# A change to the first pair of images, and to the place of three additions, in a normalised-attention block in f32

## What is computed

```python
y = group_norm(x)                             # 32 groups, no affine part
q, k = conv1x1_bn(y, qw, ...), conv1x1_bn(y, kw, ...)   # 8 heads of 32
v4 = conv1x1_bn(y, vw, ...)                   # 8 heads of 128
vl = depthwise_3x3(v4) * lv_s + ...           # 9 taps per channel
attn = q @ k.T * 32**-0.5 + ab                # per image and head, 196 x 196
attn = mix_heads(attn, th1w) + th1b           # 8 x 8 over the heads
attn = softmax(attn)
attn = mix_heads(attn, th2w) + th2b
o = relu(attn @ v + vl)
out = x + conv1x1_bn(o, pw, ...)
```

## Time and profile before

| what | us |
|---|---|
| median of the 3 runs (lowest, highest) | 4620.49 (4615.77, 4624.45) |
| the profiled execution: its own time | 4580.5 |
| its span, first to last instruction | 4578.4 |
| PE busy in the span | 4526.2 |
| DVE (VectorE) busy | 4213.5 |
| ACT (ScalarE) busy | 3571.4 |
| POOL (GpSimd) busy | 1437.7 |

### The profile page before, as it was taken

How to read it: one execution, slowest core, us unless ns; L and a number is a source line. 1 busy time by engine, 2 the same in 40 slices (tenths; PEclk the granted TensorE clock), 3 DMA queues, 4 the chain that set the end, 5 groups by cost and what they waited for, 6 DMA issues and landing times.

```text
span 4578.4 us, 108323 instructions
## 1 busy us (share of the span) xinstructions
PE 4526.2 (99%) x33666; PEld 4504.7 (98%) x33666; DVE 4213.5 (92%) x10012; ACT 3571.4 (78%) x8508; POOL 1437.7 (31%) x1285
## 2 busy tenths in 40 slices
PE   6999999999999999999999999999999999999999
PEld 6999999999999999999999999999999999999999
DVE  8999999999999999999999999999999999999998
ACT  5877878778787787787877877878778777787786
POOL 3323233233332332323323323233233332332322
PEclk8999999999999999999999999999999999999999
DMA  3223222222232222322222223222222232222322
GB/s 91 77 67 96 64 80 81 75 84 67 77 96 64 80 80 69 91 64 80 86 74 80 76 68 96 64 80 85 73 82 69 75 96 64 80 80 71 89 64 75
DMA packets 210732, 356.04 MB, mean 78 GB/s; under 512 B 15842, under 2 KB 132690, under 8 KB 210644
## 3 DMA queue, kind: packets, MB, share of 16 engines
q1 hardware_dynamic: 210708, 355.74, 26.7%
HBM read 199.70 MB, written 155.98 MB: 78 GB/s over the span
## 4 chain that ended last, share of the span: by engine, by line
PE 95%; DVE 4%; issue 1%; DMA 0%; DVEq 0%; ACT 0%; POOL 0%; POOLq 0%
PE psA L289 44%; PE psA L418 13%; PE psL L289 13%; PE psM L289 10%; PE psM L396 8%; PE psL L396 6%; DVE psC L687 1%; DVE shared L687 1%; DVE shared L778 1%; DVE probs L742 0%; PE psA L302 0%; DVE xs L664 0%; DVE q_lo L709 0%; DMA xs<-in_x 0%; DVE probs L717 0%
## 5 line engine op out<-in xcount | busy, mean ns | idle before, releaser
L687 DVE SCALAR_TENSOR_TENSOR psC<-vpad,par,psC 128x406 f32<-128x406 f32 x3072 | 1804.4, 641 | 0.0
L576 ACT ACTIVATE probs<-probs,nmax 112x196 f32<-112x196 f32 x1792 | 803.1, 450 | 120.8 <-DVE nmax L742 112.6
L289 PE MATMUL psA<-x_hi,w_lo 128*128 128x392 f32 x2304 | 794.6, 345 | 15.5 <-DVE x_lo L668 15.5
L289 PE MATMUL psA<-x_hi,w_hi 128*128 128x392 f32 x2304 | 785.9, 341 | 0.0
L289 PE MATMUL psA<-x_lo,w_hi 128*128 128x392 f32 x2304 | 784.9, 341 | 0.0
L418 PE MATMUL psA<-qa,shared 105*128 105x196 f32 x4096 | 710.1, 332 | 16.2 <-DVE shared L778 8.2
L418 PEld LDWEIGHTS psA<-qa,shared 105*128 105x128 f32 x4096 | 677.7, 191 | 35.3 <-DVE shared L778 35.2
L841 POOL TENSOR_TENSOR k_lo<-qk,k_hi 128x392 fp32r<-128x392 f32 x128 | 160.1, 1250 | 1669.3 <-ACT k_hi L482 1669.3
L709 DVE SCALAR_TENSOR_TENSOR q_lo<-qk,th,q_hi 128x392 fp32r<-128x392 f32 x1024 | 618.8, 633 | 0.0
L453 ACT ACTIVATE o_hi<-shared 128x392 fp32r<-128x392 f32 x512 | 271.7, 531 | 426.4 <-DVE shared L778 426.3
L478 ACT ACTIVATE q_hi<-qk,th 128x392 fp32r<-128x392 f32 x1024 | 594.8, 618 | 2.1
(11 more groups left out here) (83 smaller groups left out, 10804.0 us busy)
## 6 DMA issues: line engine op xcount, KB each, us to landing
by_key<-probs SPq DMA_DIRECT2D x512, 224.0 KB, 3.6
qa<-by_key SPq DMA_DIRECT2D x128, 448.0 KB, 4.3
qk<-by_key SPq DMA_DIRECT2D x128, 448.0 KB, 7.0
xs<-in_x SPq DMA_DIRECT2D x64, 588.0 KB, 5.1
shared<-in_x SPq DMA_DIRECT2D x64, 588.0 KB, 3.8
out<-shared SPq DMA_DIRECT2D x63, 588.0 KB, 3.0
qa<-in_wqkv SPq DMA_DIRECT2D x3, 768.0 KB, 8.1
stage_wp<-in_wp SPq DMA_DIRECT2D x1, 1536.0 KB, 10.5
```

The lines of the kernel that those rows point to most:

```text
L289: last = nc.tensor.matmul(dst, w, r, start=(begin and n == 0), stop=(end and n == 2))
L576: nc.scalar.activation(row, row, ACT.Exp, bias=nmax[:, img, b:b + 1], scale=-1.0, accum_out=rowsum[:, img, b:b + 1]).then_inc(s_exp, 1)
L687: nc.vector.scalar_tensor_tensor(a if tap == 7 else sums, src, taps[:, c, TAPS[tap]:TAPS[tap] + 1], a if tap == 0 else sums, MUL, ADD).the ...
```

## The change

It touches the first pair, and two orders in the loop.

- The qkv weights are loaded and split in three parts by column instead of by row: value tiles 0 to 3, then queries and keys, then value tiles 4 to 7. All three w_lo are on VectorE: the first ahead of x_lo, the others behind the constants. PE waits for each part where it first uses it. ScalarE makes x_hi ahead of the third part's w_hi.
- Two steps of the first reciprocal deviation go from GpSimd to VectorE, a third falls away (one instruction adds and subtracts).
- The memset of probs is cut to the pad columns of 112 partitions and stands at GpSimd's beginning; the row of ones comes by a transfer ahead of the projection weights.
- In the first pair VectorE makes the last eight q_lo ahead of the first transpose.
- wp_lo is made in eight instructions, each behind a step of scores, ahead of the normalisation of the next pair.
- In all pairs VectorE has a tap behind scores 0 and 1 too (`if n:` is gone); the order of the taps among themselves is the same.
- In all pairs but the first, GpSimd adds residuals 0 and 1 ahead of the mixing weights and residual 2 behind them.

```diff
--- before.py
+++ after.py
@@ -147,7 +147,7 @@
         o_tiles = out.rearrange("(t i) (p k) n -> t k p i n", i=2, p=P)
 
 
-        s_w = [sem(f"s_w{kt}") for kt in range(CT)]
+        s_w = [sem("s_w_v0"), sem("s_w_qk"), sem("s_w_v4")]
         s_wp, s_par, s_gconst = sem("s_wp"), sem("s_par"), sem("s_gconst")
         s_x, s_res = sem("s_x"), sem("s_res")
         s_store = sem("s_store")
@@ -172,6 +172,8 @@
         s_vt_out, s_ones_in, s_raw = sem("s_vt_out"), sem("s_ones_in"), [sem("s_raw0"), sem("s_raw1")][:2]
         s_eps, s_bias, s_rstd, s_xlo, s_mixw = sem("s_eps"), sem("s_bias"), sem("s_rstd"), sem("s_xlo"), sem("s_mixw")
 
+        W_PARTS = [slice(4 * P, 8 * P), slice(0, 4 * P), slice(8 * P, 12 * P)]
+
         block = ctx.enter_context(nc.Block())
         OUTS = 16 * 2 * QUADS
         N_PAR_DMA = 6
@@ -224,13 +226,15 @@
 
             load_x(0)
             sp.dma_start(same[:, :], A["same"]).then_inc(s_gconst, 16)
-            w_rows = A["wqkv"].rearrange("(p k) m -> k p m", p=P)
-            for kt in range(CT):
-                sp.dma_start(stage_w[:, kt, :], w_rows[kt]).then_inc(s_w[kt], 16)
+            w_rows = A["wqkv"].rearrange("(p k) m -> p k m", p=P)
+            for n, cols in enumerate(W_PARTS):
+                sp.dma_start(stage_w[:, :, cols], w_rows[:, :, cols]).then_inc(s_w[n], 16)
             for dst, src in ((par[:, :], A["par"]), (th1[:, :, :], A["th1"]), (small[:, :], A["small"]),
                              (abx[:, :], A["abx"]),
                              (mixw[HP:HP + 1, 0, :, :], A["th2b"]), (mixw[HP:HP + 1, 1, :, :], A["th2b"])):
                 sp.dma_start(dst, src).then_inc(s_par, 16)
+            sp.dma_start(probs[HP:HP + 1, :, :, :].rearrange("p i b n -> p (i b n)")[:, 0:TURNED_AT],
+                         A["ones"][:, 0:TURNED_AT]).then_inc(s_ones_in, 16)
             sp.dma_start(stage_p, A["wp"].rearrange("(k p) m -> p k m", p=P)).then_inc(s_wp, 16)
 
             def residual(t):
@@ -331,7 +335,7 @@
             def step(t, first, last):
 
                 if first:
-                    pe.wait_ge(s_wlo, CT)
+                    pe.wait_ge(s_wlo, 1)
                 pe.wait_ge(s_xhi, t + 1)
                 pe.wait_ge(s_xlo, t + 1)
                 for m in range(2):
@@ -340,6 +344,8 @@
                     qkv_tile(m, 4 + m).then_inc(s_v_mm, 1)
                     if first and m == 0:
                         bias_table()
+                if first:
+                    pe.wait_ge(s_wlo, 2)
                 for m in range(4):
                     if m < 2:
                         pe.wait_ge(s_v_sb, VT * t + m + 1)
@@ -351,6 +357,8 @@
                         pe.wait_ge(s_v_sb, VT * t + m - 1)
                     else:
                         pe.wait_ge(s_qk_sb, 4 * t + m + 1)
+                    if first and m == 4:
+                        pe.wait_ge(s_wlo, 3)
                     qkv_tile(m, 4 + m).then_inc(s_v_mm, 1)
                 if first:
                     pe.wait_ge(s_v_sb, VT)
@@ -382,7 +390,7 @@
                 if not first:
                     project(t, 2, True)
 
-                pe.wait_ge(s_ones_in, 16 * (t + 1))
+                pe.wait_ge(s_ones_in, 16 * (t + 2))
                 for use, (img, n) in enumerate(USES):
                     if use < 4:
                         pe.wait_ge(s_score, 28 * t + 22 + 2 * use)
@@ -399,7 +407,7 @@
                                                   start=True, stop=True)
                     mm.then_inc(s_mix_mm, 1)
                 if first:
-                    pe.wait_ge(s_wplo, 1)
+                    pe.wait_ge(s_wplo, VT)
                 else:
                     pe.wait_ge(s_pout, 3 * t)
                 if not last:
@@ -430,14 +438,14 @@
                 act.wait_ge(s_xn, 2 * (p + 1))
                 nc.scalar.copy(x_hi[:, :, :, :], xs[:, :, :, :]).then_inc(s_xhi, 1)
 
-            def weights_high(kt):
-                act.wait_ge(s_w[kt], 16)
-                nc.scalar.copy(w_hi[:, kt, :], stage_w[:, kt, :]).then_inc(s_whi, 1)
+            def weights_high(n):
+                act.wait_ge(s_w[n], 16)
+                nc.scalar.copy(w_hi[:, :, W_PARTS[n]], stage_w[:, :, W_PARTS[n]]).then_inc(s_whi, 1)
 
             weights_high(0)
             weights_high(1)
+            x_high(0)
             weights_high(2)
-            x_high(0)
 
             def conv_centre(t, c):
 
@@ -647,27 +655,32 @@
                 dve.wait_ge(s_msq, 2)
                 nc.vector.tensor_scalar(mv[:, :, :], mv[:, :, :], RUN * SUM_SCALE, None, MUL).then_inc(s_mv, 1)
 
-            def first_moments():
+            def first_deviation():
 
                 dve.wait_ge(s_gsum_mm, 1)
                 nc.vector.tensor_copy(gs[:, :, :].rearrange("p i s -> p (i s)"), psA[:, 1, 0:4]).then_inc(s_gs, 1)
-
-            def weights_low(kt):
-                dve.wait_ge(s_whi, kt + 1)
-                nc.vector.tensor_tensor(w_lo[:, kt, :], stage_w[:, kt, :], w_hi[:, kt, :].bitcast(f32),
-                                        SUB).then_inc(s_wlo, 1)
+                dve.wait_ge(s_gs, 1)
+                nc.vector.tensor_tensor(g_msq[:, :], gs[:, :, 0], gs[:, :, 0], MUL).then_inc(s_gmsq, 1)
+                dve.wait_ge(s_gmsq, 1)
+                nc.vector.scalar_tensor_tensor(g_sub[:, :], gs[:, :, 1], EPS, g_msq[:, :], ADD, SUB).then_inc(s_gsub, 1)
+
+            def weights_low(n):
+                dve.wait_ge(s_whi, n + 1)
+                nc.vector.tensor_tensor(w_lo[:, :, W_PARTS[n]], stage_w[:, :, W_PARTS[n]],
+                                        w_hi[:, :, W_PARTS[n]].bitcast(f32), SUB).then_inc(s_wlo, 1)
 
             first_stats()
-            first_moments()
+            first_deviation()
             dve.wait_ge(s_rstd, 1)
             for i in range(2):
                 nc.vector.tensor_scalar(xs[:, i, :, :], xs[:, i, :, :], gs[:, i, 0:1], rstd[:, i:i + 1], SUB, MUL).then_inc(s_xn, 1)
             weights_low(0)
-            weights_low(1)
             dve.wait_ge(s_xhi, 1)
             nc.vector.tensor_tensor(x_lo[:, :, :, :], xs[:, :, :, :],
                                     x_hi[:, :, :, :].bitcast(f32), SUB).then_inc(s_xlo, 1)
             constants()
+            weights_low(1)
+            weights_low(2)
             dve.wait_ge(s_biasmm, 1)
             nc.vector.tensor_scalar(bias[:, :], psC[0:HP, 0, 0:WINDOW], th1b, None, ADD).then_inc(s_bias, 1)
 
@@ -726,11 +739,15 @@
                     convs(1)
                 if not first:
                     dve.wait_ge(s_mix_mm, 14 * t)
+                if first:
+                    mixed_low(8)
                 turn(0)
                 convs(2)
-                mixed_low(3)
+                if not first:
+                    mixed_low(3)
                 turn(1)
-                mixed_low(5)
+                if not first:
+                    mixed_low(5)
                 convs(6)
                 for n in range(RES):
                     if n == TURNED_ROW // 2:
@@ -750,8 +767,7 @@
                         if not first:
                             dve.wait_ge(s_mixw, 8 * t)
                         nc.vector.reciprocal(rinv[:, 0, :], rowsum[:, 0, :]).then_inc(s_rinv, 1)
-                    if n:
-                        convs(1)
+                    convs(1)
                 convs(3)
                 dve.wait_ge(s_exp, 28 * t + 28)
                 nc.vector.reciprocal(rinv[:, 1, :], rowsum[:, 1, :]).then_inc(s_rinv, 1)
@@ -759,7 +775,7 @@
                 convs(64)
 
                 if first:
-                    dve.wait_ge(s_wplo, 1)
+                    dve.wait_ge(s_wplo, VT)
                 else:
                     dve.wait_ge(s_proj_mm, 3 * t)
 
@@ -786,6 +802,8 @@
         @block.gpsimd
         def _(pool):
             nc.gpsimd.memset(vpad[:, :, :], 0.0).then_inc(s_zero, 1)
+            nc.gpsimd.memset(probs[0:HP, :, :, :].rearrange("p i b (r w) -> p (i b r) w", w=PITCH)[:, :, RES], 1.0
+                             ).then_inc(s_ones, 1)
 
             def reciprocal_deviation(p):
 
@@ -793,7 +811,7 @@
                 nc.gpsimd.tensor_tensor(g_msq[:, :], gs[:, :, 0], gs[:, :, 0], MUL).then_inc(s_gmsq, 1)
                 nc.gpsimd.tensor_tensor(g_var[:, :], gs[:, :, 1], eps[:, :], ADD).then_inc(s_gvar, 1)
                 wait_alone(pool, s_gmsq, p + 1)
-                wait_alone(pool, s_gvar, p + 1)
+                wait_alone(pool, s_gvar, p)
                 nc.gpsimd.tensor_tensor(g_sub[:, :], g_var[:, :], g_msq[:, :], SUB).then_inc(s_gsub, 1)
                 wait_alone(pool, s_gsub, p + 1)
                 nc.gpsimd.tensor_tensor(rstd[:, :], g_sub[:, :], mhalf[:, :], ALU.pow).then_inc(s_rstd, 1)
@@ -828,10 +846,8 @@
                                             MUL).then_inc(s_mixw, 1)
 
             pool.wait_ge(s_eps, 1)
-            reciprocal_deviation(0)
-            nc.gpsimd.memset(probs[:, :, :, :], 1.0).then_inc(s_ones, 1)
-            pool.wait_ge(s_whi, CT)
```

(22 more changed lines are left out.)

## The result

| | before | after |
|---|---|---|
| median of 5 runs (lowest, highest), us | 4619.01 (4610.81, 4624.45) | 4535.64 (4534.58, 4536.11) |
| profiled execution, span | 4578.4 | 4532.8 |
| mean TensorE clock granted | 0.997 | 0.999 |

The change makes the kernel faster: ratio 0.9821, interval 0.9807 to 0.9835, 83 us. I had forecast 4587, with 4574 as the low end. The direction was right and the size was not. The spans differ by only 45.6, so a second thing has to be found: the median run of the kernel before lies 39 us above its own profiled execution (4580.5), that of the kernel after only 1 us above its own (4534.58).

The account below looks back on a forecast made before the run. TensorE (PE), busy 99%, was taken as the bound; gains of 8.6 + 6.5 + 17.6 + 0.8 = 33.5 us took 4580.5 to 4547.0, and 40 carried over gave 4587 us; range 4580 to 4597, 8 in 10 within 4574 to 4609.

Parts of the forecast that it names:

- Start: Up to PE's first projection: without two GpSimd instructions beside xs, PE begins at 14.5 instead of 23.11; gain 8.6 us.
- First pair: First pair of images: q_lo and wp_lo reordered, taps end sooner, pair ends 100.7 against 107.53; 6.5 us taken.
- two first taps of channels 4 and 5: First pair, VectorE: at 69.8 and 72.2 they fall inside GpSimd's normalisations and are held 1.2 and 1.5 us.
- the q_lo order: First pair: eight q_lo ahead of the transposes start PE 2.5 us earlier, but first score comes at 57.3 instead of 54.79.
- Loop: Loop pairs: a tap earlier and residuals moved bring the first addition forward; 0.28 us in 63 pairs, 17.6 us.
- The stall: Loop, attention times values: PE's weight loads wait for VectorE's addition, losing about 0.31 us per pair.
- The carried difference: Whole kernel: the runs' median lies 40 us above the profiled execution, unexplained, and was added to the forecast unchanged.
- pair 1: Loop pair with a single longer wait of 0.95, a residual holding two first taps to 2.01; losing it gains 0.8 us.
- R1: Loop: residuals run 0.2 us later than placed, the lock eats the tap, nothing won there; 4605 us, chance 0.25.
- R2: Loop: each first tap waits a whole GpSimd instruction, 1.37 us late in 63 pairs; slower, 4690 us, chance 0.05.
- R3: First pair: PE waits cold for mixing weights, VectorE's taps are held, only 1.5 us gained; 4592 us, chance 0.10.
- R4: Start: weight parts land so late that PE starts no earlier than 18, 5 us less gain; 4592 us, chance 0.05.

Follow-up runs that it names:

- e9: Changed kernel with the whole memset of probs back on GpSimd behind the first deviation, without the small memset and transfer of ones: 4539.59 us.
- e11: Changed kernel with the old place of the last eight q_lo (three between the transposes, five behind): 4533.51 us.
- e1: Kernel before, run again without any edit: 4629.53 us, ratio 1.0001, span of the profiled execution 4628.3.
- e2: Kernel before with only the new order of residuals (0 and 1 ahead of the mixing weights, 2 behind): 4578.28 us, ratio 0.9890.
- e5: Changed kernel run again without any edit, beside the kernel before on the same chip: 4535.58 us, ratio 0.9798.
- e7: Kernel before with one more GpSimd instruction, a memset of 256 elements of an unused tile ahead of the third residual: 4577.60 us, ratio 0.9888.

## Why the prediction was right and wrong

**Start, 8.6 forecast, 9.5 measured.** Right, step by step: xs 1.08 (0.8 forecast), deviation on VectorE, w_lo, x_lo, PE. Of the 0.9 above the forecast 0.8 is the weights' earlier landing, where I had only allowed for a later one; e9 shows the memset's part. The strided memset took 0.76 us and not 0.35, in GpSimd's idle time.

**First pair, 6.5 forecast, 9.6 measured.** The step that failed: "two first taps of channels 4 and 5 ... fall inside the normalisations: held 1.2 and 1.5". They took 0.70 and 0.64 in the middle of it, and the normalisation its usual 4.65. I had read the hold from rows in which GpSimd ran a `tensor_tensor`, and the normalisation is a `tensor_scalar`. Without these 2.7 the forecast's own sum, 6.8, becomes 9.5. The rest held: 4.18 of wait for q_lo (4 forecast), 4.56 for the mixing weights (5), taps of channels 6 and 7 free, next pair at 88.46 (92 less those 2.7 and the 0.9 of the start). That the q_lo order is worth nothing was nearly right; e11 shows no gain from it.

**Loop, 17.6 forecast, 25 measured in an undisturbed execution.** The stall was mis-sized at 0.31; it was 0.41, since the stage runs in 10.49 and not in 10.56 to 10.6. And VectorE came 0.43 earlier, not 0.31: the lock held the moved first taps 0.05 and 0.1 (0.68 and 0.75 long at 2168.63 and 2169.79), not 0.24 in all.

**The carried difference, 40 us, was the failure that left the range.** Of the 51.4 us between 4587 and 4535.6, 38.9 lie here (40 carried, 1.1 left between the runs of the kernel after and its profiled execution), 7.6 in the loop, 3.1 in the first pair, 0.9 in the start and 0.8 in the second held pair. The prediction put it as "no row says why, and I carry the difference over". It was no property of the chip that both kernels share, but of the kernel before: what e1 shows. The row was there: the pair that I called pair 1, two taps in 2.01 and PE's wait of 0.95, which I priced once, at 0.8. Those 0.8 times 63 are 50, more than the whole difference between runs and profile. So the two residuals moved ahead, entered as a cost, are the largest gain of the change: 50.9 alone (e2), of 93.7 for all of it (e5). In the result above 83.4 - 45.6 = 37.8 us come from it; at 0.81 per pair these are 47 pairs more than the two of the profiled execution, so the residual would have come first in about three pairs of four. Those runs were not profiled, and this share is inferred, not shown. What tips the start of two instructions that lie 0.02 us apart one way or the other, and why the first profile was on the good side in all but two pairs, is open. The low end of my range, 4574, was not worked out either: the working shown leads to 4583 less 4.

**Rivals.** R1 and R2 had the right mechanism at the wrong place: the lock did decide, but in the kernel before. R2's "whole instruction" per tap did not come. R3 and R4 did not come: the first pair gained more than forecast, and PE started at 13.63, not at 18.

The Trainium skill's rule (SBUF — State Buffer, "Who interferes with whom") that the first to issue has the shared ports and the second is blocked fits where both GpSimd's instruction and the tap have two inputs: a tap took 5.1 us under wp_lo and 1.45 under a residual (0.65 when free), and whoever starts first blocks the other, as e1 and e7 show from both sides. By the same section a VectorE instruction with two SBUF inputs meets any GpSimd instruction that reads SBUF; here the normalisation, one tensor input from SBUF, did not hold the taps, and there the measurement decides. Whether it is the number of inputs or the operation that makes the difference, no run here separates.

## What to carry to other kernels

When timed runs and the profiled execution of one kernel differ by more than their scatter, look in the profile for a stall that occurs in one or two iterations and multiply it by their number: the runs may pay it every time. Two instructions of VectorE and GpSimd that share the SBUF ports and start together by the timetable should be moved apart on purpose, by order or even by an idle instruction; which of them is first decides whether the wait falls on the engine with slack. An instruction moved off that meeting can be worth far more than its own duration, so price each move by what it stops meeting as well as by what it meets.

## What the runs showed of the hardware that I had not expected

- The hold depends on GpSimd's instruction: under a tensor_tensor (two inputs) a two-input tap took up to 5.1 us instead of 0.65; a memset of 5.0 us held a one-input tensor_scalar from SBUF to SBUF (5.72 for two of 0.5); two tensor_scalar on GpSimd, 4.65 us, held no two-input tap (0.70 and 0.64).
- The order of two starts 0.02 us apart can stay the same for nearly a whole loop (held in 2 of 63 pairs in one execution, in all 63 in another), and makes pairs of 70.67 or 71.47 us, at the same clock (0.997): spans 4578.4 and 4628.3 of the same kernel.
- One memset more on an idle engine made the kernel 1.1% faster (ratio 0.9888, 0.9873 to 0.9903).
